# Converting the first weights of a feed-forward stage two pieces a step inside the last attention steps

## What is computed

```python
x = x + xattn(layernorm(x), ctx)           # quantise both, then einsum('emk,enk->emn')
h = layernorm(x)
scores = sigmoid(h @ gate_w)               # 32 experts in 4 groups; 2 groups are masked
weights, experts = top 6 of the masked scores, weights normalised to sum 1
expert_out = sum_k weights_k * (silu(h @ w_gate[e_k]) * (h @ w_up[e_k])) @ w_down[e_k]
shared = silu(h @ sw_gate) * (h @ sw_up) @ sw_down      # inner width 1408
out = x + expert_out + shared
```

## Time and profile before

| | us |
|---|---|
| median of 3 runs (lowest, highest) | 6870.7 (6869.9, 6882.28) |
| the profiled execution | 6891.71 |
| its span in the trace | 6889.9 |
| PE busy | 6476.5 (94% of the span) |
| POOL busy | 3161.2 (46%) |
| DVE busy | 1745.4 (25%) |
| attention ends, first feed-forward tile starts | about 841 and 884.8 |

### The profile page before, as it was taken

How to read it: one execution, slowest core, us unless ns; L and a number is a source line. 1 busy time by engine, 2 the same in 40 slices (tenths; PEclk the granted TensorE clock), 3 DMA queues, 4 the chain that set the end, 5 groups by cost and what they waited for, 6 DMA issues and landing times.

```text
span 6889.9 us, 89555 instructions
## 1 busy us (share of the span) xinstructions
PE 6476.5 (94%) x32230; PEld 3067.5 (45%) x32231; DVE 1745.4 (25%) x2938; ACT 961.0 (14%) x1308; POOL 3161.2 (46%) x2065
## 2 busy tenths in 40 slices
PE   3666789999999999999999999999999999999998
PEld 1333334444444444444444444444444444444443
DVE  7999630001111111111111111111111111115555
ACT  2333301111111111111111111111111111110000
POOL 2434644336444464444654446444564465442222
PEclk9888899999999999999999999999999999999999
DMA  2333459996555565555655556555565556558877
GB/s 88 131 131 134 160 170 337 332 254 174 140 139 141 150 166 156 146 142 138 163 155 152 141 150 166 154 148 141 149 167 152 139 164 171 142 147 253 256 258 227
DMA packets 1146762, 1175.26 MB, mean 171 GB/s; under 512 B 867297, under 2 KB 867297, under 8 KB 1146721
## 3 DMA queue, kind: packets, MB, share of 16 engines
q10 hardware_dynamic: 902352, 477.20, 29.5%
q1 hardware_dynamic: 184464, 487.80, 21.6%
q0 software_dynamic: 59904, 209.75, 8.5%
HBM read 647.63 MB, written 327.16 MB: 141 GB/s over the span
## 4 chain that ended last, share of the span: by engine, by line
PE 84%; DVE 6%; DMA 4%; issue 3%; POOL 1%; DVEq 0%; ACT 0%; ACTq 0%; SPq 0%; POOLq 0%
PE ps_gu L633 55%; PE ps_d L633 25%; DMA hT<-hid_hl 3%; PE ps_d L774 2%; PE ps_d L772 2%; DMA wts<-in_ctx 1%; DVE wts L1126 0%; DVE wts L1082 0%; DVE amax L1065 0%; DVE xin L1089 0%; DVE wts L1170 0%; DVE wts L1140 0%; POOL wts L477 0%; DVE max_rows L1069 0%; DVEq L1082 0%
## 5 line engine op out<-in xcount | busy, mean ns | idle before, releaser
L633 PE MATMUL ps_gu<-wts,xT 128*128 128x512 f16 (+1 forms) x19584 | 3930.2, 362 | 9.2 <-DVEq L1386 4.0
L633 PEld LDWEIGHTS ps_gu<-wts,xT 128*128 128x128 f16 x19584 | 1895.0, 98 | 2040.4 <-issue 121.8
L633 PE MATMUL ps_d<-wts,hT 128*128 128x512 f16 x8160 | 1818.0, 381 | 36.3 <-DMA hT<-hid_hl 36.3
L474 POOL TENSOR_SCALAR wts<-stage 128x1408 f16<-128x1408 f32 (+1 forms) x476 | 586.6, 1232 | 2238.6 <-PE ps_d L774 2215.6
L1298 DVE SCALAR_TENSOR_TENSOR hid<-ps_gu,sil 128x704 f32<-128x704 f32 x272 | 242.5, 892 | 4583.1 <-ACT sil L955 4583.1
L477 POOL TENSOR_TENSOR wts<-stage,wts 128x1408 f16<-128x1408 f32 (+1 forms) x476 | 1232.0, 2588 | 39.7
L633 PEld LDWEIGHTS ps_d<-wts,hT 128*128 128x128 f16 x8160 | 800.4, 98 | 996.9 <-DMA hT<-hid_hl 31.5
L475 POOL TENSOR_SCALAR stage<-stage 128x1408 f32<-128x1408 f32 (+1 forms) x476 | 624.4, 1312 | 0.0
L955 ACT ACTIVATE sil<-ps_gu 128x704 f32<-128x704 f32 x272 | 205.9, 757 | 2847.8 <-PE ps_gu L633 2847.8
L977 ACT ACTIVATE dout<-ps_d 128x1024 f32<-128x1024 f32 x240 | 245.8, 1024 | 2184.3 <-DMA xT<-xin 1959.8
L633 PE MATMUL ps_d<-wts,xin 128*128 128x512 f16 x1536 | 383.5, 412 | 77.2 <-DVE xin L1089 54.2
(11 more groups left out here) (162 smaller groups left out, 2060.6 us busy)
## 6 DMA issues: line engine op xcount, KB each, us to landing
rows_d<-dout ACTq DMA_DIRECT2D x240, 512.0 KB, 3.3
xin<-rows_x ACTq DMA_DIRECT2D x211, 512.0 KB, 3.3
stage<-in_L_ffn_w_down SPq DMA_DIRECT2D x384, 256.0 KB, 3.2
stage<-in_L_ffn_w_gate SPq DMA_DIRECT2D x256, 352.0 KB, 3.2
stage<-in_L_ffn_w_up SPq DMA_DIRECT2D x256, 352.0 KB, 3.7
wts<-in_x SPq DMA_DIRECT2D x64, 512.0 KB, 3.6
rows_x<-wts SPq DMA_DIRECT2D x64, 512.0 KB, 2.9
wts<-rows_x SPq DMA_DIRECT2D x64, 512.0 KB, 7.0
```

The costliest lines, as they stand in the source:

```text
L474: g.tensor_scalar(high, raw, WSCALE, 1.0, ALU.mult, ALU.mult).then_inc(conv_step, 1)
L633: ins = nc.tensor.matmul(dst[c], left, right[c], start=(first and a == 0), stop=(last and a == 2))
```

## The change

POOL now converts two pieces a step, in steps 23 to 29, and none in steps 30 and 31 or behind them. SP loads the piece that takes a buffer right after each of the two is converted, so in steps 23 to 27 it waits for `conv_done` twice and loads two pieces. All 14 pieces are still loaded and converted, by the same instructions.

```diff
+        def pieces_in(i):
+            at = 2 * (i - (TT - CLEAD + 1))
+            return range(at, min(at + 2, CHUNKS))
...
             for i in range(TT - CLEAD + 1, TT):
                 around(i, x=i < TT - LEAD - 1, ctx=False)
-                c = STAGES + i - (TT - CLEAD + 1)
-                sp.wait_ge(conv_done, c - STAGES + 1)
-                load_piece(0, c, *half_a)
+                for c in pieces_in(i):
+                    if c + STAGES < CHUNKS:
+                        sp.wait_ge(conv_done, c + 1)
+                        load_piece(0, c + STAGES, *half_a)
 
             store_xt(TT - 1)
-            for c in range(STAGES + CLEAD - 1, CHUNKS):
-                sp.wait_ge(conv_done, c - STAGES + 1)
-                load_piece(0, c, *half_a)
...
-                split_piece(0, i - (TT - CLEAD + 1), 0)
-            for c in range(CLEAD - 1, CHUNKS):
-                split_piece(0, c, 0)
+                for c in pieces_in(i):
+                    split_piece(0, c, 0)
```

## The result

The changed kernel is slower: a median of 6908.28 us against 6874.82 for the kernel before on the same chip, 11 runs each, a ratio of 1.0049 with a 95% interval of 1.0026 to 1.0072. Weighted by the inverse squares of the widths of their intervals the three make 1.0033, some 22 us. Medians are of executions in the chip's faster state: four of the 23 of the kernel before in the second comparison, of 6974 us and more at a lower granted clock, are left out. A ratio is the one on record and can differ from the quotient of two medians by up to 0.002. The forecast was +18 us (1.0026), and its range ended at 6906.

The account below looks back on a forecast made before the run. Bound: a loop of PE's attention products and the first 4 us of DVE's step, 1.33 us of slack on DVE. 15 + 11.4 + 2 + 2 - 12.3 = +18.1 us on 6870.7 gives 6888.8 us; range 6866 to 6906.

Parts of the forecast that it names:

- Terms 1 and 2, first meeting: Step 24: late dequantisation makes DVE's quantisation run beside POOL's instructions; residual of step 25 later by +15 us (11 to 19).
- the lower bound: DVE's step 24 if POOL gets turns only at four long operations and once at the start: 14.3 us.
- Term 2, second meeting: Step 26: DVE and POOL meet again, 15 us taken (12 to 22.8); residual of step 27 +11.4 us (8 to 19).
- Third meeting: Narrow pieces in step 27: the quantisation of step 28 is 2.2 us late and stopped: +2 us (0 to 4).
- Term 3, the clock: PE's attention: two gaps make two `attend`s start at the low clock level: +2 us (0 to 4).
- Term 4, the routing: Routing after step 31: with POOL idle, DVE's operations get faster, all on the chain: -12.3 us.
- SP: Residual loads issued later, behind the second conversion: costed at nothing; as a bound +5 us, 6876 us, chance 0.05.
- The rival in which DVE waits for everything: Attention steps: DVE waits for all of POOL's work at both meetings: +32 us, 6903 us; chance 0.2.
- Only later, not stopped: Attention steps: DVE gets through between POOL's instructions, leaving only the shift: -4 us, 6867 us; chance 0.12.
- the second piece fits: Attention steps: POOL's idle 5.71 us takes the piece, only the routing gain remains: 6858 us; chance 0.08.

Follow-up runs that it names:

- the three: Three comparisons of the changed kernel with the kernel before: ratios 1.0049, 1.0004 and 1.0033.
- the second comparison: The unmodified changed kernel timed again against the kernel before: 6890.79 us against 6884.51, ratio 1.0004 (0.9974 to 1.0033).
- POOL's wait: Changed kernel, with `low_of_x2` on POOL waiting in steps 24 to 28 until DVE's quantisation has ended: first feed-forward tile 189.05 us behind the anchor, against 204.2.
- the piece in POOL's idle time: Changed kernel, with the second piece between dequantisation and `low_of_x2` in steps 24 to 28: first feed-forward tile 191.1 us behind the anchor.
- the kernel with the pieces late: One piece in steps 23 to 27, then 2, 3, 2, 2 in 28 to 31; against the kernel before: ratios 0.9987 and 0.9984.

## Why the prediction was right and wrong

**The direction and the mechanism held.** L1112 of step 24 was forecast near 719.2 and to go off with `low_of_x2`. It started at 720.46 (719.4 by the clock of the trace before, whose anchor is 1.1 us earlier), 0.17 us behind L503. The residuals of steps 25 and 27 moved and those of 26 and 28 didn't. POOL's wait removes nearly all of the meetings and leaves the lateness, the piece in POOL's idle time brings a meeting without lateness, and both move the residuals as the mechanism says.

**Terms 1 and 2, first meeting.** 18.5 us were taken from the end of the dequantisation to the end of DVE's step; it is 18.7 (720.33 to 739.06), and the residual starts 0.6 us behind that, which the forecast left out. +15 forecast, +15.9 measured. The 18.5 was the middle between two bounds, so its closeness is partly luck: the lower bound gave POOL five turns, and it had eight.

**Term 2, second meeting: the step that failed.** +11.4 forecast, +14.6 measured. The mechanism was right and the size too small, by "PE's clock may shift this by a microsecond, which would let DVE pass its small operations first; I take 15 us here". DVE passed nothing first: `low_of_x2(26)` starts 68.9 us behind the anchor in all three profiles, right behind the dequantisation, and the second meeting has the same lengths to 0.01 us as the first. So it costs 19.3 us from the end of the dequantisation to the residual, not 15, and the 18.5 of the first should have stood there. The miss would be 4.5 us, had the two steps in the kernel before taken 35.4 us as assumed; they took 36.7.

**Third meeting.** +2 forecast, +3.0 measured from residual 27 to 29.

**Term 3, the clock.** +2 forecast; the traces show no such loss. The forecast took it that two `attend`s would newly start at the low level. But the `attend`s of the kernel before ran at a mixture of the two levels too, behind waits of 3.1 us. The first 18 matmuls of the one behind residual 25, before:

```profile
727.07 7.02 PE L633 MATMUL ps_d<-wts,xin 128*128 128x512 f16 x18 [3.14 <-DVE xin L1089]
```

They took 7.02 us with 0.56 granted over them, and 5.96 with 0.67 after the gap of 12.07 us (the line at 744.04 above). Those behind residual 27 took 5.90 us at 0.67 after the second gap, against 5.74 at 0.69. From residual 29 to 31 the clock even gave 1.7 us back, which no term has: the first matmuls of the two `attend`s there took 5.62 and 5.40 us (0.71 and 0.74 granted) where they had taken 6.95 and 5.75 (0.57 and 0.69).

**Term 4, the routing.** -12.3 forecast; from residual 31 to the first tile it is 53.9 us before and 43.1 after, -10.8. DVE's operations give 12.6 us (6.9 in L1347, 3.2 in the two behind it, 2.5 in the last choice). But the store of `cols_x` on the chain took 5.65 us (5.75 and 5.59 in the other two profiles) instead of 3.67, which takes 2.0 back; the forecast had all of the gain on the chain and nothing against it. Why it is longer is open; in the kernel with the pieces late the whole stretch takes 42.7.

**SP** cost nothing, as forecast: residual loads issued between 700 and 830 us landed 4.0 to 5.8 us after their issue (5.3 to 6.3 before), and no residual's wait ended on a transfer.

**The rival in which DVE waits for everything** (+19.3 and +19.2 at the meetings) lies above what came: DVE's small operations get through in pairs, as L1200 behind L1112 and L1132 behind L1210, and the second instruction of the dequantisation (L489) holds none of them. Its total, 6903, is nearer to the measured median than the forecast's 6888.8, but not by its mechanism. "Only later, not stopped" and "the second piece fits" are excluded by the first 20 us of the trace.

**Where the measured total left the range.** The sum for the stages that change was 18.1 and the traces show 21.0. With 21.0 the forecast would have been 6891.7, inside the range, so the mis-sized term alone doesn't explain the 6908.28. Another 4.1 us are in the start: the kernel before measures 6874.82 over 11 runs where the first three gave 6870.7. The other 12.5 us stand in no step of attention or routing. The likely place is the feed-forward stage, which the prediction put at nothing and which scatters by 24 us between the profiles; the timed runs have no traces, so this isn't shown for them. The same scatter is a better reason than "its start and the profiler" for the profiled execution of the kernel before, 21 us above the median: its stage of 6005 us is the longest of the twelve, and the first profiled execution of the changed kernel (6903.02) is below its kernel's median. The range was built from the terms ("the forecast's own range, 6877 to 6901") and three runs that lay 12 us apart, and it left no room for this.

## What to carry to other kernels

Idle time of POOL isn't room for POOL work if DVE is busy in it. Here the two took turns by whole instructions: eight of the 18 operations of DVE's chain waited for a POOL instruction each, whatever their own size, and 5.3 us of work took 18.7. Put such work where DVE waits for something else, or have POOL wait for DVE's chain. And where work is put ahead of something that another engine needs, compare it with that engine's slack (here 0.76 and 1.33 us), not with the idle time behind it (5.71 us).

## What the runs showed of the hardware

- DVE operations of 2 to 8 elements a partition, 0.17 or 0.22 us long, were stretched by the rest of a POOL instruction, up to 2.89 us. Reductions, MAX8, BATCH_NORM_STATS2, RECIPROCAL and operations with a PSUM input kept their length beside the same POOL instructions (1.22, 0.18, 0.69, 0.19 and 1.22 us). The Trainium skill (GPSIMD Engine Reference, Key points) names contention for DVE instructions in a two-port mode or with two inputs in SBUF. The traces bear out the latter (L1141, 3.75 us instead of 1.23). Operations with one input in SBUF were held too (L1112, L1118, L1137), and no row shows in which mode they ran.
- POOL memsets (0.95 us each in the median, 1.14 beside DVE's quantisation) left a 1.23 us DVE operation with two SBUF inputs as it was, and two of 0.69 us grew to 1.27 and 1.40.
- The mutual waits repeat to 0.01 us: the second meeting, 51.33 us behind the first, has the same lengths.
